# Twice as many stand-in matmuls before the first load, and none after the first barrier, in an attention and mixture-of-experts layer on eight cores

## The chip, the cores and the metric

The kernel runs on one Trainium2 chip, on all 8 of its cores; cores 0 to 3 are one die and 4 to 7 the other. Each core works on one element of the batch with its own copy of all weights, and no core waits for another. The metric is the device time in microseconds (us) of the slowest core.

## What is computed

One transformer layer on x of shape (8, 4096, 1024): causal attention with 16 heads of 64 and rotary position, then a mixture of 8 experts of which 2 are taken per token, each sublayer after a layer norm and with a residual. Cut to what matters:

```python
h = layernorm(x)
q, k, v = split_heads(h @ Wq.T), split_heads(h @ Wk.T), split_heads(h @ Wv.T)
q, k = rope(q), rope(k)
probs = softmax(where(causal, q @ k.T / 8, -1e9))
x = x + (probs @ v) @ Wo.T
h = layernorm(x)
w, idx = softmax_of_top2(h @ Wg + bg)
eo = relu(h @ W1[e] + b1[e]) @ W2[e] + b2[e]        # for every expert e
x = x + layernorm(sum(w * eo[idx]) + h)
```

## The kernel before, in words

Every operation is recorded by a small builder, `Bld`. `b.op(engine, fn, rd=..., wr=...)` appends one instruction to that engine's stream. The builder orders work through `Reg` objects: an operation that writes a `Reg` waits for its last writer and for **every operation that has read it since** (`Reg.wr`). SP and POOL issue DMAs, each engine on two semaphores in turn; a DMA also waits until the one two places before it on its engine has landed. Each engine's stream is run in order, so an operation that waits holds everything behind it on its engine. The wait instructions themselves are in the loop that runs the streams (line 1025), and the profile shows SP's waits there.

The program has three stages with a barrier between them, in which each engine waits for all semaphores:

1. **Projections** (lines 240 to 386). Constants and the three weight matrices are loaded, then for each of 8 chunks of 512 tokens: load x (line 299), layer norm (`emit_ln`, sums at lines 202 and 211, broadcasts at 239 and 242), 24 groups of 8 matmuls for q, k and v (line 320), rope and transposes, and three stores.
2. **Attention** (from line 389). K and V of all tokens are loaded back by 8 DMAs on SP (line 441) and 4 on POOL (line 447); then for each chunk of queries `qt_s` is loaded (line 593), and for each pair of heads scores (line 601), exponentials (line 628), mask (line 633) and the product with V (line 637) run.
3. **Experts** (from about line 700). 16 half experts for each of 4 blocks of 1024 tokens, matmuls at lines 798 and 825, and a last layer norm.

The change touches the start of stage 1 and the start of stage 2.

At the start of stage 1, POOL loads `ones_b` (line 279, it writes `R_const`), DVE sets `vst` to one (line 277) and one row of `kst` to zero (line 281, it writes `R_warm`). Then PE runs 64 matmuls of one row of ones by 512 zeros into PSUM bank 7 (line 283). Nothing reads their result; each reads `R_const` and `R_warm`. Behind them in program order stand seven loads on SP (line 289: `ones_r`, `ones_c`, `id_f`, `cs_tab`, `ss_tab`, `p2s`, `epss`), and three on POOL (line 292: `wq_s`, `wk_s`, `wv_s`). All ten **write the same `R_const`**, so the first one waits for the readers recorded so far and each later one waits for the one before it. The load of x (line 299) is behind the seven on SP.

At the start of stage 2, directly behind the barrier, PE runs 16 matmuls of one row of 128 ones by 128 ones into bank 7 (line 390). They read `R_const`, which nothing writes any more. Behind them on PE stands the first scores matmul.

```python
    for wi_ in range(64):
        b.op("pe", (lambda: lambda e: e.matmul(
            bank[7][:, :], ones_b[0:1, 0:128], kst[0:1, 0:512],
            start=True, stop=True))(),
             rd=(R_const, R_warm))
    for dst, src in ((ones_r, onesd), (ones_c, onescd), (id_f, idd),
                     (cs, ctabd), (ss, stabd), (p2s, p2d), (epss, epsd)):
        b.op("sp", (lambda d, s: lambda e: e.dma_start(d[:, :], s))(dst, src),
             wr=(R_const,))
```

Of the kernel before, what the change touches and what calls it, by code (L numbers as in the profile page):

```python
# [127 lines left out]
def build(S):  # L128
# [43 lines left out]
    b = Bld()  # L172

    ones_r = nc.alloc_sbuf_tensor("ones_r", [1, 128], F32)
    ones_b = nc.alloc_sbuf_tensor("ones_b", [1, 128], BF16)
# [4 lines left out]
    bank = [nc.alloc_psum_tensor(f"bank{i}", [128, 512], F32) for i in range(8)]  # L180
# [14 lines left out]
    R_const = Reg()  # L195
# [83 lines left out]
    b.op("pool", lambda e: e.dma_start(ones_b[:, :], onesd), wr=(R_const,))  # L279
    R_warm = Reg()  # L280
    b.op("dve", lambda e: e.memset(kst[0:1, 0:512], 0.0), wr=(R_warm,))
    for wi_ in range(64):
        b.op("pe", (lambda: lambda e: e.matmul(
            bank[7][:, :], ones_b[0:1, 0:128], kst[0:1, 0:512],
            start=True, stop=True))(),
             rd=(R_const, R_warm))
# [10 lines left out]
    for tc in range(NT):  # L297
# [10 lines left out]
        for dc in range(8):  # L308
# [3 lines left out]
                 rd=(R_xin[xb], R_bank[3]), wr=(R_tm0[sl],))  # L312
            b.op("dve", (lambda dc, sl: lambda e: e.tensor_add(  # L313
                ln1[:, dc * T:(dc + 1) * T], tm0[sl][:, :], bank[2][:, :]))(dc, sl),
                 rd=(R_tm0[sl], R_bank[2]), wr=(R_ln1[dc],))
# [55 lines left out]
        for i in range(24):  # L371
            if i + 1 < 24:
# [5 lines left out]
             rd=tuple(R_qst), wr=(R_qsp[tc],))  # L378
# [3 lines left out]
             rd=tuple(R_kst), wr=(R_ksp[tc],))  # L382
# [3 lines left out]
             rd=tuple(R_vst), wr=(R_vsp[tc],))  # L386

    b.barrier()
    for wi_ in range(16):
        b.op("pe", (lambda: lambda e: e.matmul(  # L390
            bank[7][:, 0:128], ones_b[0:1, 0:128], ones_b[0:1, 0:128],
            start=True, stop=True))(),
             rd=(R_const,))
    cur[0] = FREE0
    kt_s = salloc("kt_s", [128, 8 * S], BF16)
    vh_s = salloc("vh_s", [128, NKT * 1040], BF16)
# [43 lines left out]
    for hp in range(8):  # L440
        b.op("sp", (lambda hp: lambda e: e.dma_start(
            kt_s[:, hp * S:(hp + 1) * S], k_sp[hp * 128:(hp + 1) * 128, :]))(hp),
             rd=tuple(R_ksp), wr=(R_kts[hp],))
    ng = (NKT + 7) // 8
    for g in range(ng):
# [5 lines left out]
             rd=tuple(R_vsp), wr=tuple(R_vhs[g * 8:g * 8 + n]))  # L451
# [136 lines left out]
    for qc in range(NT):  # L588
# [7 lines left out]
             rd=(R_qsp[qc],), wr=(R_qts,))  # L596
        pending_norm = []
        for hp in range(8):
# [13 lines left out]
            for kt in range(nk):  # L612
# [9 lines left out]
                for hs in range(2):  # L622
# [7 lines left out]
                         rd=(R_bank[bi],), wr=(R_prs[slot],))  # L630
                    if kt >= 4 * qc:
# [4 lines left out]
                             rd=(R_mks,), wr=(R_prs[slot],))  # L636
# [4 lines left out]
                        start=(kt == 0), stop=(kt == nk - 1)))(kt, slot, h, pa, nk)  # L641
# [8 lines left out]
            for hs in range(2):  # L650
# [8 lines left out]
                     rd=(rpa,), wr=(R_rrs[hs], R_attf[hs]))  # L659
                b.op("dve", (lambda aslice, pa: lambda e: e.tensor_copy(  # L660
                    aslice, pa[0:64, :]))(aslice, pa),
                     rd=(rpa, R_attf[hs]), wr=(areg,))
                b.op("act", (lambda rr, rr_l: lambda e: e.activation(
                    rr, rr_l, AF.Exp, scale=-1.0))(rr, rr_l),
                     rd=(R_rrs[hs],), wr=(R_rrx,))
# [96 lines left out]
    for cc in range(NCC):  # L762
# [4 lines left out]
             rd=tuple(all_l2sp), wr=(R_ln2c,))  # L767
        b.op("sp", (lambda cc: lambda e: e.dma_start(
            wrow8[:, :], wt_sp[:, cc * CC:(cc + 1) * CC]))(cc),
             rd=tuple(all_wtsp), wr=(R_wrow8,))  # L770
        b.op("dve", lambda e: e.tensor_copy(wrow8b[:, :], wrow8[:, :]),
             rd=(R_wrow8,), wr=(R_wrow8b,))
# [336 lines left out]
```

How the kernel before makes its waits and increments, by code:

```python
            def run(engobj):  # L1021
                incsz = {s: 16 for s in DMASEMS}
                for ws, fn, inc in b.stream[eng_name]:
                    for s, v in ws:
                        engobj.wait_ge(sems[s], v)
                    if fn is not None:
                        ins = fn(engobj)
                        if inc is not None:
                            ins.then_inc(sems[inc], incsz.get(inc, 1))
```

## Time and profile before

| | us |
|---|---|
| timed runs | 8407.3 and 8603.48, median 8505.39 |
| the profiled execution: its time | 8411.31 |
| its span, slowest core (core 0) | 8409.8 |
| its spans, all cores | 8364.8 to 8409.8 |

The profiled execution's span begins with core 0's first instruction and ends with its last; 1.5 us of its time lie around it. PE is TensorE's matmuls, PEld its weight loads, DVE is VectorE, ACT ScalarE, POOL GpSimd and SP SyncE; an engine's name with a q (SPq) is its instruction queue. PEclk is the granted TensorE clock as a share of 2.4 GHz, so 1.00 is 2.4 GHz and 0.50 is 1.2 GHz. A merged row of the time line gives the start, the time from there to the end of the last of its instructions, the operation, how many, and in brackets the idle time before it and what ended it.

### The profile page before, as it was taken

The page shows a single profiled execution, that of the slowest core. Times are in us where ns is not written, and L with a number is a line of the kernel's source. Part 1 is how long each engine was busy: PE and PEld are TensorE (multiplying, and loading weights), DVE is VectorE, ACT ScalarE, POOL GpSimd, SP SyncE. Part 2 cuts the span into 40 slices and gives each one's busy share as a digit, 9 for nine tenths or more (in the row PEclk, how much of TensorE's full clock was granted, in tenths as well). Part 3 has the DMA queues.
Part 4 walks back from the last instruction along what each step waited for, and adds up shares of the span by engine and source line. Part 5 has one row for each costly group of instructions (what it writes and reads, how often), then busy time and mean ns, then how long its engine had stood idle before and what let it go on. Part 6 is the DMA issues. An engine that isn't in the chain of part 4 may idle for free.

```text
span 8409.8 us, 135067 instructions; the slowest of 8 cores (8364.8 to 8409.8 us)
## 1 busy us (share of the span) xinstructions
PE 6717.9 (80%) x42544; PEld 4187.2 (50%) x42544; DVE 2734.1 (33%) x6502; ACT 2696.4 (32%) x5409; POOL 180.0 (2%) x210
## 2 busy tenths in 40 slices
PE   4777736777778787769999599998599996799995
PEld 1222212222222222257777277777377774577773
DVE  2555534332322222223232322222332222322323
ACT  0111133446557585412222222221222221322222
POOL 0000000000000000000000000000000000000000
PEclk9888856778788798789999699999799998899996
DMA  3111131121020111153343333343243343243331
GB/s 71 41 51 51 36 111 38 38 46 31 16 46 21 26 26 31 28 91 67 61 80 62 86 63 64 61 81 66 65 80 62 62 80 71 62 80 61 66 56 56
DMA packets 315648, 481.87 MB, mean 57 GB/s; under 512 B 74485, under 2 KB 132214, under 8 KB 313702
## 3 DMA queue, kind: packets, MB, share of 16 engines
q0 software_dynamic: 209280, 308.97, 21.1%
q1 hardware_dynamic: 105702, 164.26, 5.9%
q8 instruction: 389, 6.37, 0.3%
q14 instruction: 277, 2.27, 0.1%
HBM read 697.87 MB, written 75.76 MB: 92 GB/s over the span
## 4 chain that ended last, share of the span: by engine, by line
PE 67%; DVE 14%; DMA 7%; issue 7%; ACT 5%; DVEq 1%; ACTq 0%; SPq 0%; POOLq 0%; POOL 0%
PE bank L798 19%; PE bank L825 18%; PE bank L637 9%; DVE acc L869 6%; PE bank L601 4%; PE bank L320 4%; PE bank L211 2%; PE bank L481 2%; ACT pr L628 2%; DMA l2f<-ln_sp 2%; PE bank L202 2%; ACT h_s L807 1%; PE bank L336 1%; DMA wo_dc<-wot 1%; PE bank L525 1%
## 5 line engine op out<-in xcount | busy, mean ns | idle before, releaser
L825 PE MATMUL bank<-hs_s,w2h 128*128 128x256 bf16 x16384 | 2222.2, 273 | 236.3 <-DVE hs_s L811 94.6
L798 PE MATMUL bank<-ln2c,w1h 128*128 128x256 bf16 x16384 | 2131.8, 274 | 22.7 <-DMA ln2c<-ln_sp 22.7
L807 ACT ACTIVATE h_s<-bank,b1s 128x256 bf16<-128x256 f32 x2048 | 971.4, 474 | 2950.9 <-PE bank L798 2947.6
L825 PEld LDWEIGHTS bank<-hs_s,w2h 128*128 128x128 bf16 x16384 | 1544.5, 98 | 631.2 <-issue 457.9
L798 PEld LDWEIGHTS bank<-ln2c,w1h 128*128 128x128 bf16 x16384 | 1597.9, 98 | 237.4 <-issue 30.0
L811 DVE TENSOR_TENSOR hs_s<-h_s,wb_s 128x256 bf16<-128x256 bf16 x2048 | 593.8, 291 | 2783.6 <-ACT h_s L807 2640.9
L628 ACT ACTIVATE pr<-bank 128x512 bf16<-128x512 f32 x2304 | 1217.2, 596 | 402.1 <-PE bank L637 213.8
L637 PE MATMUL bank<-pr,vh_s 128*65 128x512 bf16 x2304 | 943.5, 440 | 268.4 <-ACT pr L628 137.0
L637 PEld LDWEIGHTS bank<-pr,vh_s 128*65 128x65 bf16 x2304 | 246.6, 115 | 838.8 <-issue 835.8
L869 DVE TENSOR_TENSOR acc<-bank,acc 128x512 f32<-128x512 f32 x960 | 595.2, 682 | 143.3 <-PE bank L825 72.0
L601 PE MATMUL bank<-qt_s,kt_s 64*128 64x512 bf16 x2304 | 532.1, 433 | 67.1 <-DMA qt_s<-q_sp 67.1
L633 DVE TENSOR_TENSOR pr<-pr,mk_s 128x512 bf16<-128x512 bf16 x512 | 216.1, 425 | 898.4 <-ACT pr L628 880.2
L601 PEld LDWEIGHTS bank<-qt_s,kt_s 64*128 64x128 bf16 x2304 | 134.6, 94 | 457.2 <-issue 434.3
L481 PE MATMUL bank<-att_s,wo_dc 128*128 128x512 bf16 x512 | 171.7, 509 | 86.4 <-DMA wo_dc<-wot 85.4
L232 ACT ACTIVATE rows<-rows,epss 1x512 f32<-1x512 f32 x16 | 11.5, 720 | 640.4 <-DVE rows L231 640.4
L202 PE MATMUL bank<-xin,ones_c 128*1 128x512 f32 x128 | 71.1, 720 | 166.4 <-DMA wv_s<-wvt 84.5
L920 PE MATMUL bank<-sq,ones_c 128*1 128x256 f32 x256 | 73.7, 418 | 161.9 <-DVE sq L916 159.7
L211 PE MATMUL bank<-sq,ones_c 128*1 128x512 f32 x256 | 152.5, 702 | 58.1 <-DVE sq L208 53.7
L320 PE MATMUL bank<-ln,wq_s 128*128 128x512 bf16 x512 | 154.9, 435 | 53.4 <-DVE ln L313 53.4
L332 ACT ACTIVATE qraw<-bank 128x512 f32<-128x512 f32 x128 | 76.4, 597 | 375.3 <-PE bank L320 375.3
L993 PE MATMUL bank<-id_f,y2w 128*128 128x128 f32 x256 | 94.9, 446 | 126.8 <-DVE y2w L985 125.8
L481 PEld LDWEIGHTS bank<-att_s,wo_dc 128*128 128x128 bf16 x512 | 60.9, 124 | 196.4 <-issue 176.3
(113 smaller groups left out, 3597.4 us busy)
## 6 DMA issues: line engine op xcount, KB each, us to landing
w1h<-w POOLq DMA_DIRECT2D x64, 2048.0 KB, 13.9
w2h<-w POOLq DMA_DIRECT2D x64, 2048.0 KB, 21.7
xin<-xT SPq DMA_DIRECT2D x8, 2048.0 KB
wo_dc<-wot POOLq DMA_DIRECT2D x64, 256.0 KB, 6.0
xy<-xT SPq DMA_DIRECT2D x8, 2048.0 KB
y_sp<-xy SPq DMA_DIRECT2D x64, 256.0 KB
ln_sp<-xy SPq DMA_DIRECT2D x64, 256.0 KB
l2f<-ln_sp SPq DMA_DIRECT2D x16, 1024.0 KB
```

What stands on the lines that cost most here:

```text
L202: mms = [(lambda xa, dc: lambda e: e.matmul(bk2[0:1, 0:width], ones_c.ap(), xa, start=(dc == 0), stop=(dc == 7)))(x_ap[dc], dc) for dc in ...
L211: fn = (lambda dc, sl: lambda e: e.matmul(bk2[32:33, 0:width], ones_c.ap(), sqB[sl][:, 0:width], start=(dc == 0), stop=(dc == 7)))(dc, sl)
L320: mms = [(lambda kc, dc, wsb, g: lambda e: e.matmul(bank[g][:, :], wsb[:, kc * 1024 + dc * 128:kc * 1024 + (dc + 1) * 128], ln1[:, kc * T: ...
L481: mms = [(lambda kc, dc, g: lambda e: e.matmul(bank[g][:, :], wo_dc[dc % 2][:, kc * 128:(kc + 1) * 128], att_s[:, kc * T:(kc + 1) * T], st ...
L601: fn = (lambda kt, hs, bi, hp: lambda e: e.matmul(bank[bi][:, :], kt_s[hs * 64:hs * 64 + 64, hp * S + kt * 128:hp * S + (kt + 1) * 128], q ...
L628: b.op("act", (lambda bi, slot: lambda e: e.activation(pr_s[slot][:, :], bank[bi][:, :], AF.Exp, scale=0.125))(bi, slot), rd=(R_bank[bi],) ...
L637: fn = (lambda kt, slot, h, pa, nk: lambda e: e.matmul(pa[0:65, :], vh_s[:, kt * 1040 + 65 * h:kt * 1040 + 65 * h + 65], pr_s[slot][:, :], ...
L798: mms = [(lambda dc, fc, buf, ts, hb: lambda e: e.matmul(bank[4 + hb][:, 0:TS], w1h[buf][:, dc * 1024 + fc * 128:dc * 1024 + (fc + 1) * 12 ...
L807: b.op("act", (lambda hb, e_, fcg: lambda e: e.activation(h_s[hb][:, :], bank[4 + hb][:, 0:TS], AF.Relu, bias=b1s[:, e_ * 16 + fcg:e_ * 16 ...
L811: b.op("dve", (lambda hb, ts: lambda e: e.tensor_mul(hs_s[hb][:, :], h_s[hb][:, :], wb_s[ts][:, :]))(hb, ts), rd=(R_h[hb], R_wb[ts]), wr=( ...
L825: fn = (lambda dc, fc, buf, hb, bi, half, stop, st0, ts: lambda e: e.matmul(bank[bi][:, half * 256:half * 256 + TS], w2h[buf][:, fc * 1024 ...
L869: fn = (lambda d, s: lambda e: e.tensor_add(d, s, d))(dst_ap, src_ap)
```

## The change

The number of stand-in matmuls ahead of the first load goes from 64 to 128, and the 16 behind the first barrier are taken out. Nothing else differs.

```diff
@@ -279,7 +279,7 @@
     b.op("pool", lambda e: e.dma_start(ones_b[:, :], onesd), wr=(R_const,))
     R_warm = Reg()
     b.op("dve", lambda e: e.memset(kst[0:1, 0:512], 0.0), wr=(R_warm,))
-    for wi_ in range(64):
+    for wi_ in range(128):
         b.op("pe", (lambda: lambda e: e.matmul(
             bank[7][:, :], ones_b[0:1, 0:128], kst[0:1, 0:512],
             start=True, stop=True))(),
@@ -386,11 +386,6 @@
              rd=tuple(R_vst), wr=(R_vsp[tc],))
 
     b.barrier()
-    for wi_ in range(16):
-        b.op("pe", (lambda: lambda e: e.matmul(
-            bank[7][:, 0:128], ones_b[0:1, 0:128], ones_b[0:1, 0:128],
-            start=True, stop=True))(),
-             rd=(R_const,))
     cur[0] = FREE0
     kt_s = salloc("kt_s", [128, 8 * S], BF16)
     vh_s = salloc("vh_s", [128, NKT * 1040], BF16)
```

## Rows read from the trace of the kernel before

**Rows 1.** Time line of core 0, from 0 to 125 us, all engines
```profile
1.99 3.52 DVE L277 MEMSET vst<- 128x4160 bf16 x1 [1.99 <-PEq L136]
5.56 0.48 DVE L281 MEMSET kst<- 1x512 bf16 x1
6.19 27.46 PE L283 MATMUL bank<-kst,ones_b 1*128 1x512 bf16 x64 [6.19 <-DVE kst L281]
...
33.75 0.35 SPq L289 DMA_DIRECT2D ones_r<-onesd  x1
...
61.49 0.38 SPq L299 DMA_DIRECT2D xin<-xT  x1
64.31 0.92 POOL L292 DMA_DIRECT2D wq_s<-wqt  x1 [62.10 <-DMA epss<-epsd]
...
118.19 7.05 PE L202 MATMUL bank<-xin,ones_c 128*1 128x512 f32 x12 [84.54 <-DMA wv_s<-wvt]
```

**Rows 2.** Waits of SP's queue, 0 to 135 us: total, times, longest (us)
```profile
SPq L1025 <- PE bank L283: 30.3, 1, 30.3
```

**Rows 3.** Chain that ended last, 0 to 200 us: start, length (us), what
```profile
6.19 27.48 PE bank L283 x64
33.75 1.33 DMA ones_r<-onesd
...
102.74 15.32 DMA wv_s<-wvt
118.19 8.78 PE bank L202 x16
...
163.45 1.73 PE bank L320 x8
```

**Rows 4.** Weight loads on PEld, 118 to 126 us, one for each matmul
```profile
119.00 0.13 PEld L202 LDWEIGHTS bank<-xin,ones_c 128*1 128x1 f32 x1 [0.72 <-issue]
119.85 0.13 PEld L202 LDWEIGHTS bank<-xin,ones_c 128*1 128x1 f32 x1 [0.72 <-issue]
...
122.07 0.09 PEld L202 LDWEIGHTS bank<-xin,ones_c 128*1 128x1 f32 x1 [0.39 <-issue]
122.50 0.08 PEld L202 LDWEIGHTS bank<-xin,ones_c 128*1 128x1 f32 x1 [0.34 <-issue]
```

**Rows 5.** Stretches (us): length, busy us (instructions) per engine, PEclk, DMA share, GB/s
```profile
0.00:33.70 33.70, 27.46 (x64) 9.18 (x64) 4.01 (x2) 0.00 (x0) 0.85 (x5) 1.00 0.00 0
170.00:180.00 10.00, 10.00 (x40) 4.53 (x39) 7.60 (x13) 2.39 (x4) 0.00 (x0) 1.00 0.00 0
1060.00:1070.00 10.00, 3.67 (x14) 1.60 (x12) 3.82 (x19) 0.60 (x1) 0.00 (x0) 0.69 0.27 104
1070.00:1072.00 2.00, 0.00 (x0) 0.01 (x1) 0.00 (x0) 0.00 (x0) 0.00 (x0) 0.50 0.06 20
1072.00:1074.00 2.00, 1.86 (x16) 1.61 (x16) 0.00 (x0) 0.00 (x0) 1.78 (x2) 0.50 0.44 57
1230.00:1250.00 20.00, 11.86 (x32) 2.84 (x32) 9.67 (x17) 10.04 (x18) 0.00 (x0) 0.50 0.46 158
1250.00:1270.00 20.00, 14.65 (x49) 4.37 (x48) 8.91 (x16) 11.13 (x20) 1.75 (x2) 0.79 0.08 15
```

**Rows 6.** Time line of core 0 around the first barrier, 1063.5 to 1150 us
```profile
1071.67 33.33 SPq L441 DMA_DIRECT2D kt_s<-k_sp  x8
...
1072.02 1.86 PE L390 MATMUL bank<-ones_b 1*128 1x128 bf16 x16 [6.31 <-DMA v_sp<-vst]
...
1128.52 0.39 SPq L593 DMA_DIRECT2D qt_s<-q_sp  x1
...
1135.77 1.03 PE L601 MATMUL bank<-qt_s,kt_s 64*128 64x512 bf16 x4 [61.89 <-DMA qt_s<-q_sp]
```

**Rows 7.** Long stretches of core 0, same columns as group 5
```profile
1131.00:4400.00 3269.00, 2568.41 (x12342) 1200.07 (x12343) 976.93 (x2155) 1581.59 (x3019) 80.39 (x93) 0.82 0.21 42
```

**Rows 8.** Spans and mean granted clock by core
```profile
core 0: 8409.8 us, clock 0.875
...
core 2: 8364.8 us, clock 0.879
```

## The prediction

> **What bounds the kernel now.** PE carries most of the chain over the whole span, but the change sits in two short places where PE does no useful work, so averages say little; each place is read from its own stretch. I read three views. The time line of the first 125 us says what runs, and its brackets say what ended each idle time [rows 1]. SP's waits and the chain that ended last say whether the stand-in matmuls are cover for something or are themselves on the path [rows 2, 3]. The stretches around the barrier, with the time line there, say the same for the second place [rows 5, 6].
>
> What the reader is to see at the start: the 64 stand-in matmuls run from 6.19 to 33.65 us, and until then no load but `ones_b` has been issued. SP's first load goes out at 33.75, directly behind the last of them [rows 1]. That is no coincidence of order: SP's queue has a wait of 30.3 us that PE's line 283 ends [rows 2]. The reason is in the builder: the load of `ones_r` writes `R_const`, all 64 matmuls read it, and a writer waits for all readers. From there everything is a single file, since all ten loads write the same register: seven on SP, then `wq_s` on POOL at 64.31, which waited for `epss`, then `wk_s`, then `wv_s`, which lands at 118.06 (102.74 and 15.32), and only that starts the first matmul with a use, line 202 at 118.19 [rows 1, 3]. The load of x stands on SP behind the seven, at 61.49, so it is late with them. So the matmuls at line 283 are a term of the start, 27.48 us of it [rows 3], with nothing beside them that could take up a delay.
>
> At the barrier: PE starts the 16 short matmuls at 1072.02 and is done with them 1.86 us later, at 1073.88. It then waits for `qt_s` until 1135.77, 61.89 us [rows 6]. `qt_s` is issued at 1128.52 on SP, behind the eight loads of K that went out from 1071.67 on, and none of these reads or writes anything of line 390.
>
> **Part one, 64 more matmuls of 512 columns.** The price of one is its share of the train: 27.48 / 64 = 0.429 us [rows 3], or, from the time at which the train is under way, 512 columns at 1.2 GHz, 0.427. Sixty-four more cost 64 x 0.427 = **27.3 us**. Nothing covers them: SP's ten loads in file and x all start later by this sum, and line 202 with them. The queues held up are SP (seven constants, x, and every later store and load), POOL (three weight loads), and through them PE, DVE and ACT in full. DVE's two fills are ahead of the train and do not move. No later step has slack against the start of stage 1, since each stage hangs on the end of the one before through a barrier; so the 27.3 us arrive undiminished at the end.
>
> **The clock of that train.** The profile grants 1.00 in this stretch [rows 5], which would be 2.4 GHz, but the pitch says otherwise: 512 columns in 0.429 us is 1.2 GHz, while eight matmuls of the same width in a stretch at 1.00 take 1.73 us, 0.216 each [rows 3, 5]. The train thus ran at the lower level for all of its 27 us. The very same stretch of 1.00 holds at line 202 a step that can be seen: weight loads 0.85 us apart at 119, and 0.43 apart at 122.5 [rows 4]. So the clock did rise there, under matmuls that fill all 128 rows, and the train of single rows had not raised it. I take the 1.00 of the first 120 us for a value that stands before the record has an event, and go by the pitch. If the second 64 ran like the stretch at 1.00, they would cost 64 x 0.216 = 13.8 us; I keep this as the lower end. There is no end above 0.429, as both levels are then spent.
>
> The Trainium skill has a rule that bears on this, in "TensorE: Matmul & The Clock Gate", Part 1, "What's actually happening": the throttled state is the default and PE's activity releases it. By that rule most of the train, and all of the second half, would be at the fast level, the added part would cost the 13.8 us and line 202 could begin fast. The trace contradicts it for matmuls of one row: no matmul of the 64 is faster than the first. It agrees at line 202.
>
> **What a longer train could give back.** The most it could bring is a PE that is fast at line 202 from the start. There about four and a half matmuls run at 0.856 in place of 0.428, so 1.9 us. But between the train and line 202 PE is idle for 84.54 us [rows 1], and that does not change; at the barrier an idle time far shorter than that let the clock fall (0.69 in the stretch to 1070, 0.50 from there) [rows 5]. I take 0, with 1.9 as the bound.
>
> **Part two, 16 matmuls of 128 columns less.** They take 1.86 us and are followed by 61.89 us of waiting for a load [rows 6]; what is gone becomes waiting, and the gain is 0. The bound from below is 0 as well, for the load chain behind `qt_s` never sees them. If the cover were gone (if `qt_s` were there) they would be worth 1.86 us. Their other possible worth is the clock. They ran at 0.50 (1.86 / 16 = 0.116 each, near 128 columns at 1.2 GHz), and the granted clock is 0.50 before them, in them and up to 1250, where the attention's own matmuls raise it [rows 5]. So the first 115 us of attention work run at the low level with them already; without them there is nothing to lose. Value taken: 0.
>
> **The sum.** 27.3 + 0 - 0 = 27.3 us on the profiled execution's own 8411.3 us (span 8409.8 and 1.5 around it), so **8438.6, rounded 8439 us**, a ratio of 1.0032. The two timed runs lie 196 us apart, 8407.3 and 8603.5; the profiled execution stands 4 us over the lower one and 94 us under their median of 8505.4. The sum starts from the profiled one, so it is to be compared with the lower run: by the median, the same 27.3 us would give 8532.7. It is 0.3%, far inside the 2% which a measurement of this kernel can tell from no change.
>
> **Rivals.**
> - *The train rises to the fast clock in its second half.* For it: the same matmul in a warm stretch takes 0.216. Against it: 64 of 64 at 0.427. 8411.3 + 13.8 = 8425; with the 1.9 at line 202, 8423. Chance 0.05. The Trainium skill's page named above leads to this case.
> - *The transfers hide the train anyway*, if the loads do not wait for it. For it: the load engines are idle, share 0.00, up to 33.7 us [rows 5], so there would be all the room. Against it: the 30.3 us wait and the issue at 33.75 [rows 1, 2]. It gives 8411. Chance 0.03.
> - *Slower by over 2%: the 16 matmuls after the barrier held something up in PE's clock that attention lives on.* Attention runs at a mean of 0.82 over 3269 us [rows 7]; at two levels that is (0.82 - 0.5) / 0.5 = 0.64 of the time fast, 2092 us. Each fast microsecond of PE that falls to the low level costs one more. It decides from 168 us, 8% of those 2092. All of it lost would be 8439 + 2092, about 10530; a tenth, 8648. Against it: the clock stood at 0.50 for 175 us behind them, so they set nothing [rows 5]. Chance 0.03.
> - *Faster by over 2%* would need 168 + 27 us from a happier alignment of clock and gaps. The cores run one program and their spans differ by 45 us, at clocks 0.875 and 0.879 [rows 8]; so the shift of 27 us can move the end by some 20 us either way by chance, not by 195. Chance 0.01.
>
> **How the numbers follow.** Forecast 0.88, the first two rivals 0.08, the slow one 0.03, the fast one 0.01. The forecast and the two mild rivals are all within 2%, which makes 0.96; slower 0.03, faster 0.01. The likeliest case's own range is 8439 with about half the spread of the cores, 8420 to 8465. The range for the time takes in the warm rival at 8423 with a small margin, so 8415 below; above, the runs shown can put the median of two half of their 196 us higher, 8439 + 98 = 8537, and with the scatter of 20 us 8560.
>
> **What would show each step.** 128 matmuls at line 283 from 6.2 to 61.0 us at a pitch of 0.427; SP's wait for line 283 at 57.6 in place of 30.3; `ones_r` issued at 61.1 and line 202 first at 145.5 on core 0, 27.3 later each; the same cold pitch of 0.85 at the first matmuls of line 202. After the barrier (1099 in place of 1071.7) PE's wait for `qt_s` about 68 to 70 us, since the 6.31 before line 390 and the 1.86 of its matmuls join the 61.89; clock 0.50 up to about 1277. Wrong would be: a pitch near 0.216 anywhere in the train (13.8 us), a load that is issued ahead of 61 us (the sum falls towards 0), or a mean clock between the barrier and 4400 that lies under 0.80.

## The result: 0.3 to 0.4% slower, some 28 of 33 us of it at the start

| | before | changed |
|---|---|---|
| median of all timed runs, us | 8584.69 (12 runs, 8407.3 to 9075.12) | 8639.43 (14 runs, 8445.04 to 8939.38) |
| ratio of the undisturbed runs | | 1.004, 95% interval 1.0024 to 1.0056 |
| the same, second comparison | | 1.0027, interval 0.998 to 1.0074 |
| undisturbed dies, slowest core, us | 8406.0 +- 0.9 (56 dies, of the later comparisons) | 8440.4 +- 1.4 (32 dies, both comparisons) |
| line 202 starts, mean of 8 cores, us | 114.4 | 143.2 and 142.8 |

In half or more of the executions of nearly every kernel here one die, or both, ran 1 to 9% longer at a lower granted clock, so the ratios leave these runs out, and the "undisturbed dies" are those whose slowest core lies within 35 us of the lowest such value of the same kernel (mean and standard error).

The change makes the kernel slower by 34 us in the first comparison (the ratio of 1.004) and by 32 in the second (by the dies), where 27.3 was forecast. In the first it is clear of noise. The interval there, 1.0024 to 1.0056, holds the forecast ratio of 1.0032 too. The interval of the second holds 1. Both are far inside 2%.

In the profiled execution of the changed kernel, cores 0 to 3 had a lower mean clock than cores 4 to 7; the spans of cores 4 and 5 are to be compared with those of [rows 8]:

```profile
core 1: 8588.3 us, clock 0.856
...
core 4: 8450.0 us, clock 0.877
core 5: 8444.6 us, clock 0.876
```

The chain of the changed kernel's core 1 from 0 to 230 us (start, length, what) answers [rows 3]:

```profile
6.20 54.78 PE bank L283 x128
61.06 1.35 DMA ones_r<-onesd
...
125.17 14.54 DMA wv_s<-wvt
139.85 9.95 PE bank L202 x16
```

SP's waits of the same core, 0 to 200 us (total, times, longest), answer [rows 2]:

```profile
SPq L1020 <- PE bank L283: 57.5, 1, 57.5
```

The train (the row of stand-in matmuls) is 27.3 us longer (54.78, before 27.48), SP's wait for it is 27.2 longer (57.5, before 30.3) and its first load goes out 27.31 us later (61.06, before 33.75). The file of ten loads takes no less than it did: averaged over the cores, 82.2 us pass from the end of the train to line 202, where it was 80.8.

Around the barrier, the stretches and PE's waits of the changed kernel's core 4 (from 1110 and from 1090 us; the seventh column of numbers, before DMA's share, is the granted clock):

```profile
1110.00:1162.00 52.00, 0.00 (x0) 0.00 (x0) 0.00 (x0) 0.00 (x0) 4.09 (x5) 0.50 1.02 307
1162.00:1280.00 118.00, 64.13 (x169) 15.61 (x169) 60.52 (x116) 62.95 (x109) 0.00 (x0) 0.52 0.09 27
1280.00:1300.00 20.00, 11.27 (x38) 3.70 (x39) 7.27 (x13) 8.24 (x15) 1.75 (x2) 0.80 0.32 49
...
PE bank L596 <- DMA wo_dc<-wot: 70.4, 1, 70.4
```

The line 596 is the scores matmul, 601 before. One wait of 70.4 us stands where 6.31 + 1.86 + 61.89 = 70.1 stood [rows 6], and the clock is at its low level for some 118 us of attention in both [rows 5]. The releaser named is another load than before (the view puts a wait down to the one that came last), and the DMA share is at 1.02 up to the end of the wait.

### The profile page after: what moved, and what is told of

The parts are those of the page before. It is cut to its first block, busy times and chain, and to the rows that moved or that the text cites. A ratio compares the mean times of both kernels' runs of the same rounds, so it can differ in the third digit from the quotient of the medians.

```text
span 8588.3 us, 135163 instructions; the slowest of 8 cores (8416.6 to 8588.3 us)
## 1 busy us (share of the span) xinstructions
PE 6902.6 (80%) x42592; PEld 4270.1 (50%) x42592; DVE 2737.9 (32%) x6502; ACT 2696.3 (31%) x5409; POOL 179.5 (2%) x210
## 4 chain that ended last, share of the span: by engine, by line
PE 68%; DVE 14%; DMA 7%; issue 6%; ACT 5%; DVEq 1%; ACTq 0%; SPq 0%; POOLq 0%; POOL 0%
PE bank L793 19%; PE bank L820 19%; PE bank L632 9%; DVE acc L864 6%; PE bank L596 4%; PE bank L320 4%; PE bank L211 2%; PE bank L476 2%; ACT pr L623 2%; DMA l2f<-ln_sp 2%; PE bank L202 1%; ACT h_s L802 1%; DMA wo_dc<-wot 1%; PE bank L336 1%; PE bank L520 1%
## 5 line engine op out<-in xcount | busy, mean ns | idle before, releaser
L820 PE MATMUL bank<-hs_s,w2h 128*128 128x256 bf16 x16384 | 2311.2, 281 | 212.8 <-DVE hs_s L806 85.9
L793 PE MATMUL bank<-ln2c,w1h 128*128 128x256 bf16 x16384 | 2220.2, 282 | 23.7 <-DMA ln2c<-ln_sp 23.7
L820 PEld LDWEIGHTS bank<-hs_s,w2h 128*128 128x128 bf16 x16384 | 1581.8, 100 | 654.7 <-issue 444.1
L793 PEld LDWEIGHTS bank<-ln2c,w1h 128*128 128x128 bf16 x16384 | 1638.8, 101 | 280.0 <-issue 30.0
L332 ACT ACTIVATE qraw<-bank 128x512 f32<-128x512 f32 x128 | 76.4, 597 | 375.1 <-PE bank L320 375.1
```

Of the source, the lines that this page charges most:

```text
L793: mms = [(lambda dc, fc, buf, ts, hb: lambda e: e.matmul(bank[4 + hb][:, 0:TS], w1h[buf][:, dc * 1024 + fc * 128:dc * 1024 + (fc + 1) * 12 ...
L820: fn = (lambda dc, fc, buf, hb, bi, half, stop, st0, ts: lambda e: e.matmul(bank[bi][:, half * 256:half * 256 + TS], w2h[buf][:, fc * 1024 ...
```

## The experiments

Nine more kernels ran, and the changed one again, in three comparisons. Each was compared with the kernel before on its own chip. The table gives the shift of line 202's first matmul, mean of the 8 cores of the profiled execution, against 114.4 in the kernel before, and of the undisturbed dies' slowest core against the kernel before **in the same comparison** (8405.3, 8402.3 and 8408.2 us in the three). "The 16" are the short matmuls behind the barrier; "full height" means all 128 rows in place of one. The shift of line 202 is read from one execution.

| kernel | line 202, us | end, us |
|---|---|---|
| changed, again | +28.4 | +32.4 +- 2.1 |
| 128, the 16 kept | +27.6 | +28.7 +- 2.7 |
| 64, the 16 gone | +0.6 | +3.1 +- 1.9 |
| no train, the 16 kept | -29.3 | -23.0 +- 2.2 |
| 128, loads not waiting for it, no 16 | -32.2 | -24.4 +- 3.3 |
| 64 of full height | -12.7 | -8.9 +- 3.1 |
| 280 of full height behind the barrier | -0.7 | +3.3 +- 5.8 |
| 256, no 16 | +82.3 | +76.4 +- 2.9 |
| own registers, no stand-ins | -94 | -84.0 +- 5.1 |
| own registers, x one chunk ahead | -95 | -187.2 +- 3.8 |

### The two parts of the change, each alone

```diff
-    for wi_ in range(64):
+    for wi_ in range(128):
```

> Part one alone: 128 stand-in matmuls at the start, the 16 behind the barrier kept. If the loads in file are pushed back by the train (my theory), SP's wait for line 283 is 57.5 us, its first load goes out at 61.1 and the time is 27.3 us over before, a ratio of 1.0032. If the part of the measured 1.004 (some 34 us) that is over 27.3 belongs to the removal behind the barrier, this kernel shows 27.3 and the removal alone some 7 to 10. If a longer train costs something more than its length, this kernel alone shows 34 or more.

The ratio was 1.0035, interval 1.0015 to 1.0055. SP's waits on core 4, 0 to 200 us:

```profile
SPq L1025 <- PE bank L283: 57.6, 1, 57.6
```

The end moved by 28.7 +- 2.7 us, the price of the train within the error. This part is nearly all of the change.

```diff
     b.barrier()
-    for wi_ in range(16):
-        b.op("pe", (lambda: lambda e: e.matmul(
-            bank[7][:, 0:128], ones_b[0:1, 0:128], ones_b[0:1, 0:128],
-            start=True, stop=True))(),
-             rd=(R_const,))
```

> Part two alone: 64 at the start as before, none of the 16 behind the barrier. My theory: they are covered by the 62 us in which PE waits for qt_s, so 0 us, within 5 either way; PE's one wait for qt_s is some 70 us, and the clock stays 0.50 up to about 1250 us as it did with them. Rival: they held up the clock in attention; then the mean granted clock from 1131 to 4400 us falls under 0.82 and the time is 7 us or more over before.

The ratio was 0.9994 (0.9944 to 1.0045). Core 4: PE's waits from 1066 to 1145 us, and stretches:

```profile
PE bank L596 <- DMA qt_s<-q_sp: 68.4, 1, 68.4
...
1131.00:1249.00 118.00, 61.58 (x161) 14.98 (x162) 58.90 (x112) 60.26 (x105) 0.00 (x0) 0.50 0.10 28
1249.00:1269.00 20.00, 14.47 (x45) 4.44 (x45) 8.90 (x16) 10.70 (x19) 1.75 (x2) 0.83 0.07 16
1131.00:4400.00 3269.00, 2564.38 (x12313) 1197.83 (x12329) 975.59 (x2154) 1582.98 (x3019) 80.11 (x92) 0.82 0.21 41
```

The mean clock from 1131 to 4400 is 0.82, what it was with them [rows 7], and in the 118 us of early attention PE is busy for 61.58 us at a clock of 0.50. So the 16 did not hold up the clock, and the mean clock from 1131 to 4400 us is 0.82 to 0.83 on the changed kernel's cores 4 to 7, too. The end stands at +3.1 +- 1.9 us: a cost of a few us isn't excluded, and nothing in the trace shows one. The two parts add to 31.8, the whole is 32.4 and 34.

### Is it the matmuls or the wait for them

```diff
-    for wi_ in range(64):
+    for wi_ in range(0):
```

> No stand-in matmul at the start, the 16 behind the barrier kept. My theory: the train is pure delay, so the first SP load moves from 33.75 to about 4.0 us (when ones_b has landed), and the time falls by 29.7 us to a ratio of 0.9965. Rival, that the train serves the clock: then more of line 202 or the matmuls behind it run at the half pitch, and less than 29.7 comes back or the kernel is slower. The first matmuls of line 202 should show a pitch of 0.85 us, as they do with the train.

On core 4 (time line, 0 to 175 us) the first load and line 202:

```profile
3.46 0.35 SPq L289 DMA_DIRECT2D ones_r<-onesd  x1
...
80.88 9.71 PE L202 MATMUL bank<-xin,ones_c 128*1 128x512 f32 x16 [80.88 <-DMA wv_s<-wvt]
```

Against 33.75 the load is 30.3 us earlier, and line 202 is 29.3 earlier on the mean. At the end 23.0 +- 2.2 are left, 6 to 7 less than I had put down. The ratio, over few runs, was 0.9991 (0.9959 to 1.0023), which by itself shows no gain; the gain stands on the dies. The train serves nothing: line 202 takes 9.71 us for its 16 matmuls without it, and 9.92 with 128 ahead of it (the kernel with 128 and the 16 kept, same core). Over the eight cores it takes 8.5 to 10.0 us without the train, 8.5 to 9.7 with 64 and 8.3 to 10.0 with 128 or 256.

```diff
-    b.op("pool", lambda e: e.dma_start(ones_b[:, :], onesd), wr=(R_const,))
+    R_oneb = Reg()
+    b.op("pool", lambda e: e.dma_start(ones_b[:, :], onesd), wr=(R_oneb,))
...
-             rd=(R_const, R_warm))
+             rd=(R_oneb, R_warm))
```

> The changed kernel (128, and no 16), but ones_b has a register of its own that only its load writes and only the stand-in matmuls read, so no later load waits for the train. It tells the wait from the matmuls. My theory: it is the wait that costs. SP's first load goes out at about 1 to 2 us, the train of 54.8 us runs beside the loads, line 202 starts near 86 on core 0, and the time is 32 us under before (0.9962), 59 under the changed kernel. Rival, that the train's own work costs (PE busy, or what it does to the clock): the time stays near the changed kernel's 1.003 to 1.004.

Core 4, time line from 0 to 175 us:

```profile
6.20 54.77 PE L284 MATMUL bank<-kst,ones_b 1*128 1x512 bf16 x128 [6.20 <-DVE kst L282]
78.28 9.93 PE L202 MATMUL bank<-xin,ones_c 128*1 128x512 f32 x16 [17.32 <-DMA wv_s<-wvt]
...
1.07 0.35 SPq L290 DMA_DIRECT2D ones_r<-onesd  x1
```

This decides it. All 128 matmuls are there and take their 54.77 us, the first load goes out at 1.07, and line 202 starts at 78.28, with PE idle for only 17.32 us ahead of it. It starts 61 us before the changed kernel's (82.2 for 143.2 on the mean), and the kernel ends 59.6 us before it (8380.9 against 8440.5, from two comparisons). The first load goes out 60.0 us earlier: 54.8 are the train, and the other 5 the time ahead of it, since the load no longer waits for `ones_b` and the fill either. The matmuls cost nothing; that ten loads are written as if they depended on them costs their whole length.

### How the price grows, and whether a longer train gets fast

```diff
-    for wi_ in range(128):
+    for wi_ in range(256):
```

> The changed kernel with the dose doubled again: 256 stand-in matmuls at the start, none behind the barrier. The measured 1.004 stands for some 34 us, and the train adds 27.3; this tells whether a longer train costs more than its length. Theory of length alone: 192 more than before at 0.427 us, so 82 us over before, 8493 (1.0097). Rival of an extra price per matmul: 34 us for each 64, so 102 us, 8513 (1.0121). Rival that the train's clock rises at some length: a pitch of 0.216 somewhere in the 256, and less than 82.

> The changed kernel itself, beside the one with 256 on the same chip. Length alone: 27.3 us over before. If what is over that in the first comparison (some 7 us) is more than scatter, it comes again as 34 or more, and between this kernel and the one with 256 there are 54.6 us either way.

Core 4 of the kernel with 256, time line from 0 to 220 us:

```profile
6.19 109.38 PE L283 MATMUL bank<-kst,ones_b 1*128 1x512 bf16 x256 [6.19 <-DVE kst L281]
```

109.38 us for 256 is 0.427 each, the pitch of 1.2 GHz from the first to the last: the train never gets faster. Line 202 moved by 82.3 us, 0.3 off the 192 x 0.427 = 82.0, so no matmul has an extra price. At the end the kernel is 76.4 +- 2.9 over before and 44.0 +- 3.1 over the changed one on the same chip, where 54.6 went in. At line 202 the two are 53.9 apart, so about 10 us of what enters there between 128 and 256 do not arrive, while between 64 and 128 some 4 us more arrive than enter. The rival of 34 us for each 64 is refuted.

Where the difference arises can be read from the profiled executions, on the cores of undisturbed dies. From line 202 to the first scores matmul the kernel before takes 1017.8 us on the mean, and every kernel that keeps the file of loads 1014 to 1019: the shift passes stage 1 whole. From there to the last scores matmul it is 2322.6 before, 2326.3 in the changed kernel and 2324.5 with 256. Behind it, where the experts are, it is 4931.8 before, 4949.6 in the changed kernel, 4944.9 with 256, and 4931.9 with 128 and the 16 kept. The changed kernel's 17.8 us there are nearly all waits of PE (16.8 more), and 12.0 of them are one kind, the sums of the last layer norm waiting for DVE's squares. Core 4 from 3700 to 8450 us, before and changed:

```profile
PE bank L920 <- DVE sq L916: 154.7, 40, 41.5
...
PE bank L915 <- DVE sq L911: 179.7, 44, 52.6
```

The kernel with 128 and the 16 kept, whose train is as long, takes in this part what the kernel before does, so a longer train alone does not bring it. What lengthens that wait in one execution and not in another is open.

### Why the train ran slow

```diff
-    b.op("dve", lambda e: e.memset(kst[0:1, 0:512], 0.0), wr=(R_warm,))
+    b.op("dve", lambda e: e.memset(kst[:, 0:512], 0.0), wr=(R_warm,))
...
-            bank[7][:, :], ones_b[0:1, 0:128], kst[0:1, 0:512],
+            bank[7][:, :], kst[:, 0:128], kst[:, 0:512],
```

> The kernel before with the same 64 stand-in matmuls at the start, but of all 128 rows (zeros by zeros, 128x128 by 128x512) in place of one row; DVE zeroes 128 rows in place of one. It asks why the train ran at 1.2 GHz for its whole length. My reading: one row is not work that raises the clock. Then this train falls from a pitch of 0.427 to 0.216 us after some ten matmuls, as line 202 did, lasts about 16 us in place of 27.5, and the time is 11 to 12 us under before (0.9986). Rival: nothing at a program's start raises the clock within 27 us, or zeros do not; then the pitch stays 0.427 and the time that of before.

Core 0: the train in the time line, and the stretches from 6 us (the seventh column of numbers, before DMA's share, is the granted clock):

```profile
6.21 16.43 PE L283 MATMUL bank<-kst 128*128 128x512 bf16 x64 [6.21 <-DVE kst L281]
...
12.00:22.00 10.00, 10.00 (x48) 4.51 (x46) 0.00 (x0) 0.00 (x0) 0.00 (x0) 1.00 0.00 0
...
23.00:100.00 77.00, 0.00 (x0) 0.00 (x0) 1.29 (x2) 0.00 (x0) 2.67 (x3) 0.51 0.69 155
```

The same 64 matmuls on 128 rows take 16.43 us in place of 27.46. From 12 to 22 us there are 48 of them, 0.21 each, the fast level. So it was their one row that went with 1.2 GHz, not the start of the program and not the zeros. (The weights changed from ones to zeros in the same edit, which was not tried by itself.) And the clock column now falls: it reads 0.51 in the idle time behind the train. The kernel before reads 1.00 through a train at 1.2 GHz [rows 5] and through the idle time behind it, core 0:

```profile
33.70:118.00 84.30, 0.00 (x0) 0.00 (x0) 1.29 (x2) 0.00 (x0) 2.67 (x3) 1.00 0.71 151
```

So the 1.00 there is no measurement; that it is the value ahead of the first record is my reading. The end came in at -8.9 +- 3.1, for the 11.0 that the train is shorter by. Nor did this train help line 202: 82 us of waiting lie between, and its 16 matmuls took 9.78 us.

### What a real warm-up behind the barrier would bring

```diff
     b.barrier()
-    for wi_ in range(16):
-        b.op("pe", (lambda: lambda e: e.matmul(
-            bank[7][:, 0:128], ones_b[0:1, 0:128], ones_b[0:1, 0:128],
-            start=True, stop=True))(),
-             rd=(R_const,))
...
+    z2 = salloc("z2", [128, T], BF16)
+    R_z2 = Reg()
+    b.op("dve", lambda e: e.memset(z2[:, 0:512], 0.0), wr=(R_z2,))
+    for wi_ in range(280):
+        b.op("pe", (lambda: lambda e: e.matmul(
+            bank[7][:, :], z2[:, 0:128], z2[:, 0:512],
+            start=True, stop=True))(),
+             rd=(R_z2,))
```

(`z2` is a tile of zeros behind the stage's other tiles; the 64 at the start stay.)

> The kernel before, with the 16 short matmuls behind the barrier replaced by 280 of all 128 rows (zeros by zeros, 512 columns, some 62 us by a pitch of 0.216), which fill the wait for qt_s. It asks what the stand-ins behind the barrier could have brought at best. My theory: the granted clock is 1.00 up to the first scores matmul near 1136 and falls back to 0.50 soon after, since attention's first matmuls leave it at 0.50 by themselves; the time is that of before, 0 to 5 us less. Rival: a clock once raised lasts; then it stays at 1.00 from 1136 to 1250, where PE is busy for some 60 us at half pace, and up to 30 us are saved.

Core 0, the time line from 1066 us and the stretches:

```profile
1071.78 63.06 PE L413 MATMUL bank<-z 128*128 128x512 bf16 x280 [6.72 <-DVE z L411]
1135.10 0.61 PE L604 MATMUL bank<-qt_s,kt_s 64*128 64x512 bf16 x4 [0.26 <-DMA qt_s<-q_sp]
...
1100.00:1135.00 35.00, 34.84 (x162) 15.57 (x160) 0.00 (x0) 0.00 (x0) 3.21 (x4) 1.00 0.99 298
1135.00:1138.00 3.00, 1.66 (x8) 0.54 (x8) 1.27 (x3) 2.17 (x4) 0.00 (x0) 1.00 0.02 2
1138.00:1140.00 2.00, 1.98 (x7) 0.51 (x6) 1.28 (x3) 1.30 (x3) 0.00 (x0) 0.56 0.04 8
1140.00:1142.00 2.00, 1.63 (x4) 0.36 (x3) 0.85 (x2) 1.20 (x3) 0.00 (x0) 0.50 0.00 0
```

The clock stands at 1.00 up to the first scores matmul and is at 0.50 within 5 us of it; from 1142 to 1249 us PE is busy for 53.96 of 107 us, at 0.50 throughout. A warm-up that is fast up to the first scores matmul is worth 3 us of the higher level here, and no gain shows at the end (+3.3 +- 5.8). So the 16 that were removed, which ran at 0.50 [rows 5], had no more than this to bring in this place.

### A version that beats both

The stand-ins are left out in both places. Each constant and weight matrix has its own register, and its uses wait for that alone; the first chunk's x goes out second on SP and the three weight matrices first on POOL.

```diff
+    cload(ones_c, onescd, R_onec)
+    xload(0)
+    cload(ones_r, onesd, R_oner)
+    cload(epss, epsd, R_eps)
+    cload(p2s, p2d, R_p2)
...
+    wload(0)
+    wload(1)
+    wload(2)
```

> No stand-in matmuls in either place, and every constant and weight matrix on a register of its own: x for the first chunk goes out second on SP, the three weight matrices at once on POOL, and each use waits for its own load. My theory, that the single file of the loads (84 us from 33.75 to 118) is the larger part of the same wait: line 202 starts between 15 and 25 us in place of 118, and the time is 90 us under before (80 to 100), a ratio of 0.989. Rival: the loads share the same 16 engines, so what is needed first comes late and the first group of line 320 waits for wq_s; then about 30 to 60 us.

Core 0, time line from 0 to 175 us:

```profile
19.66 9.55 PE L205 MATMUL bank<-xin,ones_c 128*1 128x512 f32 x16 [19.66 <-DMA xin<-xT]
...
48.71 0.59 PE L333 MATMUL bank<-ln,wq_s 128*128 128x512 bf16 x1 [0.94 <-DVE ln L326]
```

(Line 205 is 202 before, and 333 is 320.) It starts at 19.66 in place of 118.19, and the end is 84.0 +- 5.1 us earlier. The first group of line 333 waits for DVE and not for `wq_s`, so the rival of the shared load engines falls. Against the kernel without a train, which keeps the single file, the end is 61 us earlier (84.0 less 23.0, two comparisons). Some 10 us of the gain are given back: PE's waits for the x of the seven later chunks are 91.7 us on the mean of the cores, 81.1 in the kernel before.

```diff
     for tc in range(NT):
-        if tc > 0:
-            xload(tc)
+        if tc + 1 < NT:
+            xload(tc + 1)
```

> The kernel of own registers, and each chunk's x is issued on SP one chunk ahead, in front of the stores of q, k and v that hold it up in the kernel before. PE's seven waits for xin, 81 us in total in the kernel before, should go: 70 to 80 us less than the kernel of own registers, 160 to 180 under before, a ratio of 0.980. Rival: DVE's sums of squares or the stores take the place of the wait; then half of it or less.

PE's waits of core 0, 0 to 1050 us:

```profile
PE bank L205 <- DMA xin<-xT: 19.6, 1, 19.6
```

The seven later waits are gone and nothing has taken their place. The gain, 103 us over the kernel of own registers and 187.2 +- 3.8 over the kernel before (a ratio of 0.978 by the dies), is more than forecast. The waits that went were 91.7 us and not the 81 of the kernel before. The rest goes with the granted clock: in stage 1 on core 1 it is 0.90 from 20 to 860 us, 0.85 from 118 to 1040 in the kernel before. That it is higher because PE no longer stands idle before each chunk is likely, but no run here separates the two.

## Why the prediction was right, and where it was wrong

- **The mechanism and the size at the start: right.** 27.3 us from the length of the train; measured 27.31 at the first load, and 28.8 and 28.4 at line 202. That the loads wait for the train was read from SP's wait [rows 2] and the issue time [rows 1], and the kernel whose loads don't wait shows it.
- **Arrives undiminished at the end: roughly.** The changed kernel is 32 to 34 us over before, the 128 alone 28.7. Across the kernels with the file of loads the end moved by up to 8 us more or less than line 202 did, with errors of 2 to 6 us each. The step that failed in small is "no later step has slack", so that the shift arrives undiminished: it does through stage 1 (1014 to 1019 us in every one), but behind the scores the changed kernel took 4949.6 us for 4931.8, mostly in one of PE's waits. The prediction allowed 20 us of this, from the spread of the cores [rows 8]. What lengthens that wait is open.
- **Pitch over the clock column: right.** The train of 256 and the train of full height showed both halves: one row did not raise the clock in 109 us, and the 1.00 stands over a train and an idle time alike.
- **Up to 1.9 us at line 202: a bound of core 0 only.** Its 16 matmuls took 8.8 us; on the other cores of the kernel before it is up to 9.7, so up to 2.8 us. The value taken, 0, was right: no train changed them.
- **The 16 at 0 us: right within 3 us.** The 70 us wait was as forecast; the clock as well.
- **The rivals fell**: the fast second half by a pitch of 0.427 to the last of 256, the hidden train by the 57.5 us wait, the loss of clock in attention by the mean of 0.82 before and 0.82 to 0.83 after.
- **Wrong: the time and its range.** 8439, with 8415 to 8560, does not hold the measured median of 8639.43. The step that failed is the one from the kernel's own time to a median of runs: the sum starts from 8411.3, the profiled execution, and the upper end puts half of the distance of the two times shown, 98 of 196 us, and 20 us of scatter on top. So it counted on a median between a low time and one near 8600. Of 15 executions of the changed kernel on record, 14 of which make the median, 10 took 8530 us or more, up to 8939, each with one or both dies at a lower clock; the median of all lay among them, 200 us over the sum, and that of the kernel before went to 8584.69 in the same way. The other five have their median at 8448, 9 us over the forecast of 8439. With two times 2.3% apart, the upper end should have been at least the higher one plus the shift, 8603 + 27 = 8631, and beyond it, because nothing says that the higher of two is the highest. Why a die runs at the lower clock in one execution and not in the next is not shown by any run here.
- **Luck** has no part in the 27.3: it was read from rows, and the load and line 202 moved by it. That the end came within 7 us of it is partly chance, by what the other kernels show.

## What to carry to other kernels

Before work is put in front of a program as a filler, look at what its registers make wait: an instruction whose result nobody reads still holds back every later writer of what it reads. The profile tells it in one row, a queue's wait that ends with the filler, and the cure is a register of its own for each load: with the stand-ins gone as well it brought 84 us here, where the change cost 32 to 34. And check a warm-up by the pitch of its own matmuls and by the idle time behind it: the one-row train ran at the slow level, and behind the full-height one 82 us of waiting followed, in which the clock fell to 0.51; neither warmed anything. For a forecast of a median, ask first how far apart the executions of one kernel lie.

## What the runs showed of the hardware that I had not expected

Matmuls of one row by 512 columns, back to back for 109 us, stayed at 0.427 us each, which is 1.2 GHz; the same on 128 rows ran at 0.21 from 12 us on, which is 2.4 GHz. The Trainium skill, "TensorE: Matmul & The Clock Gate", Part 1, "What's actually happening", says that the default state is throttled and activity releases it; the runs agree for 128 rows (0.21 us each from 12 us on) and contradict it for one row (0.427 us each over all 109 us). The granted clock of a profile can read 1.00 while the pitch says 1.2 GHz, here from 0 to 118 us, through the train and the idle time behind it. And a shift of 27 to 82 us at the start, which stage 1 passes on whole, came out at the end up to 8 us longer or shorter.
